# A two-layer transformer block on one core: where the first feed-forward bias is added, who makes the low parts of its hidden values, and how weights are buffered and the last stage ordered

## What is computed

```
x = x + attention(layernorm(x), ctx, mask)       # one head, masked keys
x = x + experts(layernorm(x))                     # layer 0: 4 encoder layers, each batch takes its best 2
x = x + attention16(layernorm(x), ctx)            # layer 1: 16 heads, causal
x = x + moe(layernorm(x))                         # shared expert for all, one of 8 experts for 512 tokens

encoder layer: qkv = x @ iw.T + ib ; o = softmax(q k / 4) v ; o = o @ ow.T + ob
               x = layernorm(x + o) * n1w + n1b
               ff = relu(x @ l1w.T + l1b) @ l2w.T + l2b      # 256 -> 1024 -> 256
               layernorm(x + ff) * n2w + n2b
```

## Time and profile before

| what | us |
|---|---|
| median of three runs | 782.21 (781.33 to 782.88) |
| the profiled execution, its own time | 782.31 |
| its span in the trace | 780.5 |
| PE busy in the span | 716.6 (92%) |
| DVE busy | 620.0 (79%) |
| POOL busy | 378.5 (48%) |
| ACT busy | 338.8 (43%) |
| time that ScalarE's `hh` (L1149) waited for PE | 67.8 |
| time that GpSimd's `affine2` (L2077) waited for DVE | 171.3 |

### The profile page before, as it was taken

One profiled execution on the slowest core, in us unless ns is written; L12 is line 12 of the kernel. 1 busy time (PEld: TensorE's weight loads), 2 busy tenths in 40 slices (PEclk: granted clock), 3 DMA queues, 4 the chain that ended last, 5 costly groups with the idle time before them and its releaser, 6 DMA issues.

```text
span 780.5 us, 29149 instructions
## 1 busy us (share of the span) xinstructions
PE 716.6 (92%) x11014; PEld 567.3 (73%) x11014; DVE 620.0 (79%) x1803; ACT 338.8 (43%) x711; POOL 378.5 (48%) x637
## 2 busy tenths in 40 slices
PE   5687879999999999999999999999999999987896
PEld 4466557888888888888888888888666566665684
DVE  4686665878888878888797878788889988997864
ACT  4676224343434344343434343434455555553210
POOL 4688523353535354544545353534434554547354
PEclk9797689999999999999999999999999999999798
DMA  9787200000000000000000000000112232322120
GB/s 313 253 266 274 89 2 3 3 3 3 3 3 4 3 3 3 3 3 3 3 3 4 3 3 3 3 16 10 43 57 81 78 90 90 104 89 69 38 73 7
DMA packets 24799, 40.98 MB, mean 53 GB/s; under 512 B 3871, under 2 KB 16809, under 8 KB 24411
## 3 DMA queue, kind: packets, MB, share of 16 engines
q1 hardware_dynamic: 23240, 37.13, 14.3%
q0 software_dynamic: 704, 1.71, 0.8%
q10 hardware_dynamic: 726, 0.30, 0.2%
HBM read 30.60 MB, written 8.91 MB: 51 GB/s over the span
## 4 chain that ended last, share of the span: by engine, by line
PE 69%; DVE 13%; POOL 5%; issue 4%; DMA 4%; ACT 4%; POOLq 0%; SPq 0%; ACTq 0%; DVEq 0%
PE ps L498 7%; PE ps L492 7%; PE ps L500 6%; PE ps L499 6%; PE ps L698 6%; DVE mx L1522 4%; PE ps L640 4%; PE ps L716 4%; PE ps L754 4%; PE ps L756 3%; PE ps L755 3%; DMA stage<-in_w 3%; PE ps L642 3%; PE ps L641 2%; PE ps L752 2%
## 5 line engine op out<-in xcount | busy, mean ns | idle before, releaser
L1131 ACT ACTIVATE pT<-ps 128x1024 f32<-128x1024 f32 x96 | 93.1, 1021 | 123.2 <-PE ps L698 123.2
L1522 DVE TENSOR_REDUCE mx<-ps 128x16 f32<-128x2048 f32 x48 | 109.5, 2281 | 1.0 <-PE ps L659 1.0
L2077 POOL TENSOR_TENSOR y<-y,vec 128x256 f32<-128x256 f32 x32 | 23.2, 726 | 171.3 <-DVE y L1288 171.3
L754 PE MATMUL ps<-xh,w_hi 128*128 128x128 bf16 x512 | 99.4, 219 | 0.0
L755 PE MATMUL ps<-xl,w_hi 128*128 128x128 bf16 x512 | 99.3, 219 | 0.0
L756 PE MATMUL ps<-xh,w_lo 128*128 128x128 bf16 x512 | 99.3, 219 | 0.0
L1982 POOL TENSOR_TENSOR rs<-rs,cst 128x1 f32<-128x1 f32 x132 | 75.6, 573 | 10.3
L1980 POOL TENSOR_TENSOR rs<-mv,cst 128x1 f32<-128x1 f32 x132 | 28.0, 212 | 99.7 <-DVE mv L1285 93.1
L498 PE MATMUL ps<-w_hi,hh 128*128 x256 | 69.8, 273 | 0.0
L499 PE MATMUL ps<-w_hi,hl 128*128 x256 | 69.8, 273 | 0.0
L500 PE MATMUL ps<-w_lo,hh 128*128 x256 | 69.8, 273 | 0.0
(11 more groups left out here) (361 smaller groups left out, 2436.1 us busy)
## 6 DMA issues: line engine op xcount, KB each, us to landing
stage<-in_w SPq DMA_DIRECT2D x32, 384.0 KB, 4.9
vec<-in_vec SPq DMA_DIRECT2D x4, 896.0 KB, 5.7
vec<-in_tw SPq DMA_DIRECT2D x12, 256.0 KB, 2.9
ctxc<-in_ctx SPq DMA_DIRECT2D x19, 128.0 KB, 2.2
comb<-x SPq DMA_DIRECT2D x16, 128.0 KB, 1.7
comb<-x1b SPq DMA_DIRECT2D x16, 128.0 KB
out<-x SPq DMA_DIRECT2D x16, 128.0 KB, 2.1
ytok<-t SPq DMA_DIRECT2D x14, 128.0 KB, 1.8
```

The source lines that it names most:

```text
L754: mm(dst, w(w_hi, c, j), xh[:, c, :], start=False, stop=False)
L1131: A(pT[:, 8 * a:8 * a + 8, :].rearrange("p h q -> p (h q)"), ps[:, 2 * a:2 * a + 2, :].rearrange("p g k -> p (g k)"), ACT.Exp, scale=SCALE ...
L1522: nc.vector.tensor_reduce(mx[:, :], att.rearrange("p g s k -> p (g s) k"), AX.X, ALU.max, negate=True).then_inc(m_max, 1)
```

## The change

The diff, cut to its core. "hf" is a new fp32 buffer of two halves for the hidden values after bias and ReLU; "bunit" holds the eight bias columns of a unit.

```diff
 # buffers and SyncE, first attention
+        stage_even = [vec[:, (1 + q // 2) * V_EXP + 2 * D + (q % 2) * QCH: ...] for q in range(4)]
+        def staged(i, q):
+            return stage[:, q, :] if i % 2 else stage_even[q]
             def next_quarter(i, q):
                 ...
-                sp.dma_start(stage[:, q, :], w_d[:, ds((i + 1) * ...)]).then_inc(w_in[q], 16)
+                quarter(i + 2, q)
-            for i in range(PAIRS - 1):
-                if i % 2 == 1:
-                    bias_rows(i // 2)
+            for i in range(PAIRS - 2):
+                if i == 2:
+                    sp.wait_ge(cst_ready, 1)
+                    bias_rows(0)
+                if i == 4:
+                    bias_rows(3)
                 ...
-            bias_rows(E - 1)
+            sp.wait_ge(w_lo_quarter, PAIRS - 1)
+            sp.wait_ge(w_lo_ready, (PAIRS - 1) * 3)
+            bias_rows(1)
+            bias_rows(2)
 # TensorE, hidden and second
-                    mm(dst, b1hl[:, b0:b0 + 128], row_of(e), start=True, stop=False)
                     for c in range(KC):
-                        mm(dst, w(w_hi, c, j), xh[:, c, :], start=False, stop=False)
+                        mm(dst, w(w_hi, c, j), xh[:, c, :], start=(c == 0), stop=False)
                 ...
                 if half == 1:
                     pe.wait_ge(hl_b, u + 1)
+                    pe.wait_ge(hh_a, u + 1)
+                else:
                     pe.wait_ge(hl_a, u + 1)
 # TensorE, last stage
+            def warm(n):      # n products of 512 columns into a free bank
             sh_transposes(B - 1)
+            warm(2)
             ...
             sh_z(B - 3)
+            warm(3)
             ...
             last.then_inc(d_oT, 1)
+            warm(1)
 # ScalarE, relu and its place
             def relu(u, half):
                 act.wait_ge(h_b if half else h_a, u + 1)
-                A(hh[:, 4 * half:4 * half + 4, :], ps[:, 7 - half, :]..., ACT.Relu).then_inc(hh_b if half else hh_a, 1)
+                act.wait_ge(bunit_ready, 1 + u + 1)
+                if u > 0:
+                    act.wait_ge(hl_b if half else hl_a, u)
+                for j in range(4):
+                    k = 4 * half + j
+                    last = A(hf[half][:, 128 * j:128 * j + 128], ps[:, 7 - half, 128 * j:128 * j + 128], ACT.Relu,
+                             bias=bunit[:, u % RING, k:k + 1])
+                last.then_inc(hf_ready, 1)
+                act.wait_ge(hf_ready, 16 + u * 2 + (1 if half else 2))
+                copy(hh[:, 4 * half:4 * half + 4, :], hf[half]...).then_inc(hh_b if half else hh_a, 1)
+                if attends(n):
+                    oo(n)
                 if encodes(f):
                     relu(f, 1)
-                if attends(n):
-                    oo(n)
 # VectorE
-                if encodes(f):
-                    h_low(f, 1)
             ...
-                if encodes(f):
-                    h_low(f, 0)
+                weights_quarter(i)            # now ahead of pair_stats(i + 2)
 # GpSimd
+            def h_low(u, half):
+                pool.wait_ge(hh_b if half else hh_a, u + 1)
+                tt(hl[:, 4 * half:4 * half + 4, :], hf[half]..., hh[:, 4 * half:4 * half + 4, :],
+                   ALU.subtract).then_inc(hl_b if half else hl_a, 1)
+            def unit_bias(u):
+                cols = bcols[:, ds(digit(words_pool[u // WORD], u % WORD) * B_COLS, B_COLS)]
+                nc.gpsimd.tensor_copy(bunit[:, u % RING, :], cols).then_inc(bunit_ready, 1)
             (in block)
                 if encodes(f):
                     rstd(1, n, l1_var, l1_veps, l1_rstd)
+                if encodes(n - 2):
+                    h_low(n - 2, 0)
                 ...
                     affine1(f, ex(-1))
                     x1_bias(f, 1 - slot, ex(-1))
+                if encodes(f):
+                    h_low(f, 1)
                 if encodes(n - 3):
                     rstd(2, n - 2, l2_var, l2_veps, l2_rstd)
                     affine2(n - 3, ex(-3))
+                if encodes(n + 2):
+                    unit_bias(n + 2)
 # last stage: VectorE makes last_of_equal(2) ahead of mask_tokens(3), last_of_equal(3) and
 # stored_rows ahead of mask_z(0) (before: after gated_norm(1) and gated_norm(2));
 # GpSimd gathers the rows (2, 3) of comb after the last tile's affine, not after tile 1's
```

More of the change, by code:

```diff
@@ L80 @@
 K_ALL = K_ROW + NROW
-B_QK = DFF
-B_ALL = DFF + 2 * D
+B_QK = 0
+B_ALL = 2 * D
+B_COLS = FC
+RING = 4
 def batch_of(u):
@@ L146, in encoder_kernel @@
         b1hl = sb("b1hl", [128, B_ALL], bf16)
+        bcols = sb("bcols", [128, E * B_COLS])
+        bunit = sb("bunit", [128, RING, B_COLS])
+        hf_a = sb("hf_a", [128, 512])
         cst = sb("cst", [128, C_ALL])
@@ L204, in encoder_kernel @@
         stage = sb("stage", [128, 4, QCH])
+        stage_even = [vec[:, (1 + q // 2) * V_EXP + 2 * D + (q % 2) * QCH:(1 + q // 2) * V_EXP + 2 * D + (q % 2 + 1) * QCH]
+                      for q in range(4)]
+        def staged(i, q):
+            return stage[:, q, :] if i % 2 else stage_even[q]
         kraw = vec[:, 0:K_ALL]
+        hf = (hf_a, h[:, 512:1024])
         gl = h[:, 0:12 * B * E].rearrange("p (k j) -> p k j", j=B * E)
@@ L293, in encoder_kernel @@
         x_third = c_ctx
+        w_even = (tw_in0, tw_in1, tb_in, tg_in)
+        W_EVEN = 16 * (PAIRS // 2)
         A1, D1 = B + 1, UNITS + 1
@@ L373, in _ @@
                 sp.dma_start(rows_f, b1_d[:, c0:c0 + width]).then_inc(b1_in, 16)
+            sp.dma_start(bcols[:, :], bc_d).then_inc(bcols_in, 16)
             sp.dma_start(s12_raw, sw_d[:, 0:KC * 2 * HM]).then_inc(sw_in, 16)
@@ L940, in _ @@
                 block_c(b, b % 2, ex_of(UNITS - 1)[0] if b == 1 else None)
+            def warm(n):
+                for _ in range(n):
+                    mm(ps[:, 5, :], identb[:, :],
+                       identb[:, :].rearrange("p (o k) -> p o k", o=1).broadcast_to([128, 4, 128]), start=True, stop=True)
             gathered()
@@ L1049, in weights_high @@
             def weights_high(i, q):
-                act.wait_ge(w_in[q], i * 16 + 16)
-                copy(w_hi[:, ds(i * (4 * QCH) + q * QCH, QCH)], stage[:, q, :]).then_inc(w_hi_ready, 1)
+                act.wait_ge(landed(i, q), (i // 2 + 1) * 16)
+                copy(w_hi[:, ds(i * (4 * QCH) + q * QCH, QCH)], staged(i, q)).then_inc(w_hi_ready, 1)
             def pair_exps(i):
@@ L1148, in relu @@
                 act.wait_ge(h_b if half else h_a, u + 1)
-                A(hh[:, 4 * half:4 * half + 4, :], ps[:, 7 - half, :].rearrange("p (c k) -> p c k", k=128),
-                  ACT.Relu).then_inc(hh_b if half else hh_a, 1)
+                act.wait_ge(bunit_ready, 1 + u + 1)
[7 more added lines that the diff above has]
+                act.wait_ge(hf_ready, 16 + u * 2 + (1 if half else 2))
+                copy(hh[:, 4 * half:4 * half + 4, :], hf[half].rearrange("p (c k) -> p c k", k=128)).then_inc(hh_b if half else hh_a, 1)
             def block(n, kp):
@@ L1172, in tw @@
             def tw(c, turn, j):
-                act.wait_ge(tw_in1 if j else tw_in0, turn * 16)
+                act.wait_ge(tw_in1 if j else tw_in0, W_EVEN + turn * 16)
                 copy(w_hi[:, ds(c * TCH, TCH)], tstage[:, j, :]).then_inc(tw_hi, 1)
@@ L1565, in x1_low @@
                    ALU.subtract).then_inc(x1T_split, 1)
-            def h_low(u, half):
-                dve.wait_ge(hh_b if half else hh_a, u + 1)
-                stt(hl[:, 4 * half:4 * half + 4, :], ps[:, 7 - half, :].rearrange("p (c k) -> p c k", k=128), 0.0,
-                    hh[:, 4 * half:4 * half + 4, :], ALU.max, ALU.subtract).then_inc(hl_b if half else hl_a, 1)
             def sum2(u, slot):
@@ L1827, in _ @@
             dve.wait_ge(sv_in, 32)
+            dve.wait_ge(hl_b, UNITS)
             for b in range(1, B):
@@ L1957, in _ @@
             sh_sum(B - 1)
+            last_of_equal(2)
             mask_tokens(3)
             gated(1)
+            last_of_equal(3)
+            stored_rows()
             mask_z(0)
             gated_norm(1)
-            last_of_equal(2)
             gated(2)
+            gated_norm(2)
             mask_z(1)
-            gated_norm(2)
-            last_of_equal(3)
-            stored_rows()
             for step_of, t in ((gated, 3), (mask_z, 2),
@@ L2013, in weights_low @@
                 for c in range(0, QCH, LOW):
-                    last = tt(w_lo[:, ds(w0 + c, LOW)], stage[:, q, c:c + LOW], w_hi[:, ds(w0 + c, LOW)], ALU.subtract)
+                    last = tt(w_lo[:, ds(w0 + c, LOW)], staged(i, q)[:, c:c + LOW], w_hi[:, ds(w0 + c, LOW)], ALU.subtract)
                 last.then_inc(w_lo_ready, 1)
@@ L2120, in block_c @@
                     rstd(1, b + (A1 - 1), s_var, s_veps, s_rstd)
+                if b == 1:
+                    h_low(UNITS - 1, 0)
                 if served(b + 1):
@@ L2151, in base_of @@
                 return digit(words_pool[u // WORD], u % WORD) * V_EXP
```

(2 more changed lines are left out.)

60 lines of the change are left out of this document (34 added, 26 removed).

## The result

The changed kernel takes 885.9 us (884.8 to 886.7, four runs); the kernel before took 782.1 beside it. The ratio is 1.133, 95% interval 1.131 to 1.135: slower by 104 us. The forecast was 896, the range 835 to 935.

What follows compares the result with a forecast made beforehand. PE was taken as the bound, with DVE and POOL just in time. Span 780.5 + 87 (two waits) + 36 (clock) - 6 (first attention) - 3 (last stage) = 894.5, with 1.8 around it 896 us; range 835 to 935.

Steps and rivals of the forecast that it cites:

- What bounds the kernel: Second stage: PE, busy 99.16 of 100 us, is the bound, but DVE and POOL arrive just in time.
- The bias products: TensorE, second stage: eight products fewer save at most 0.45 us a unit, 14.4 us; a good part would become waiting.
- ScalarE's half: Each relu half: four activations 1.15 us, own semaphore wait 0.1, cast 0.62; together 1.9 us against 0.60.
- The chain: From t, x1's transposes' start, through relu, h_low, rstd(2), norm2, y_low: PE waits about 2.9 us before even blocks' projection_qk.
- The second wait: Ahead of x1's transposes in every even block: PE stands still about 3.3 us, behind GpSimd's list after an odd block.
- (b): Rival: chain shorter than priced, or only one of the two stalls bites; 820 to 845 us, chance 0.12.
- The clock: Second stage: 30 idle times of 2.9 and 3.3 us lower PE's granted clock, 1.2 us each, +36 us.
- First attention: First stage: twice the buffers remove weight waits, all pairs at 7.6 us would save 9; taken -6, bounds -9 and +2.
- Last stage: Six warm products save up to 4 us, reordering up to 3, gather delays up to 2.5; taken -3, bounds -7 and +2.
- (a): Rival: the same two waits, but the clock holds; 860 us, 850 to 872, chance 0.25.
- (d): Rival: the clock stays low for most of the stage, all 81 us and dependent delays; 935 to 960 us, chance 0.08.
- (c): Rival: faster, h_low comes before norm2 is due, decided at t + 5.9; 763 us, 757 to 775, chance 0.05.

Runs made afterwards that it cites:

- low_dve: The changed kernel with both halves of h_low given back from GpSimd to VectorE, the biases staying on ScalarE: 783.1 us.
- rstd_first: The changed kernel with GpSimd's rstd(2) moved ahead of h_low(f, 1) instead of behind it: 803.1 us.
- wait_hh_a: The kernel before with one added wait: GpSimd waits for ScalarE's later half, relu(f, 0), ahead of rstd(2): 847.8 us.
- warm_fill: The changed kernel with extra TensorE products filling both stalls of every even block from block 4 on, no wait removed: 859.1 us.
- relu_plain: The changed kernel with ScalarE's four activations of 128 columns replaced by one of 512, first layer's bias left out of the computation: 859.7 us.
- no_warm: The second stage of the kernel before with the changed kernel's first and last stages, minus the last stage's six extra products: 775.5 us.
- wait_hh_b: The kernel before with one added wait: GpSimd waits for ScalarE's earlier half, relu(f, 1), ahead of rstd(2): 786.9 us.
- low0_dve: The changed kernel with only h_low(., 0) given back to VectorE, h_low(f, 1) staying on GpSimd ahead of rstd(2): 878.0 us.
- warm_proj: The changed kernel with 13 extra TensorE products ahead of projection_qk of every even block from block 4 on, none ahead of x1's transposes: 869.6 us.

## Why the prediction was right, step by step

**What bounds the kernel.** Right. DVE and POOL came just in time, and PE's 99% gave no room to either.

**The bias products** could save at most 14.4 us and gave none: nothing of the 0.45 us of a unit gets past `out_proj`, which waits for `o_low` (low_dve: at t + 6.10 as before). The prediction had "a good part"; it is all of it.

**ScalarE's half.** 1.15 us for the four activations, exactly the sum from the Exp of 128 columns; the wait for its own semaphore 0.03, not 0.1; 1.80 in all, not 1.9. GpSimd's `h_low` 1.15 (1.16), `unit_bias` 0.19 (0.3; its lower bound).

**The chain.** `hh` at t + 6.53 (predicted 6.35), `rstd(2)` ends at t + 8.53 (8.4), `projection_qk` at t + 9.91 (9.85); the wait 3.00 us (2.9). That this chain and no other makes the wait, is shown by rstd_first, which removes it by an order, and wait_hh_a, which makes it by a wait.

**The second wait**, ahead of x1's transposes: 2.55 us, predicted 3.3. The odd block is 15.83 us (416.95 to 432.78) instead of 16.3; `unit_bias` and the way from `norm2` to `affine2` are shorter. A pair with the clock held is 31.9 us (warm_fill), not 32.4: 15 × 5.3 = 80 us, not 87. Both waits are in every pair, so (b)'s case of one wait alone did not come.

**The clock: mechanism right, both factors wrong.** The term was 30 falls at 1.2 us, 36 in all. The trace of after has one fall in nearly every pair, not two: six from 300 to 500 us, with 37.5 us at half speed. The pair that starts at 296.48 has none and takes 32.3 us; the one that starts at 328.77 has two and takes 35.8. Each fall costs about twice what I took: 34.1 - 31.9 = 2.2 us, near the 2.7 of the earlier trace rows. 15 × 2.2 = 33 by the pairs, 27 by the medians of warm_fill and after. The two errors, too many falls and too cheap ones, nearly cancel: that the term came within 10 us is luck. The rule that I set beside it, that a loop which waits between bursts pays the slow clock anew after every wait (the Trainium skill, "TensorE: Matmul & The Clock Gate", section "HAM oscillation — how this bites in real kernels"), is stated there for a kernel whose waits last about 3 to 5 us, which I left out; for the shorter waits of this case it is not borne out. In wait_hh_a, with 29 waits of 1.6 to 2.4 us, the clock is at half for 3.4 of the 200 us from 300 to 500, and it falls eight times in the whole stage; in relu_plain eight of 13 pairs have a fall.

**First attention**: -3.15, predicted -6. The step that failed is "all pairs at 7.6". The maxima of pairs 0 and 7 are at 12.86 and 71.78, 8.4 us a pair instead of 8.9; only the last interval is short (4.6), most are 8.8, and the first is 10.3 where it was 7.4. The waits for weights did go: from 20 to 68 us the kernel before has this row in the view of the waits, and after the change no engine there waits for a DMA.

```profile
ACT w_hi L1032 <- DMA stage<-in_w: 16.4, 11, 3.5
```

So these waits lay mostly beside something else that sets 8.8 us a pair. What that is, no run here shows.

**Last stage**: -4.9, predicted -3. I gave the extra products up to 4 us; no_warm shows that most of the gain is the order's, and leaves 0 to 2.4 us for the products. Both ends together are worth 6 us by the medians (776.0 against 781.7), less than the 8.1 of the two traces.

**The sum** that the parts make: 780.5 + 80 + 27 - 3 - 5 = 879.5. The span is 883.0. The 80 + 27 are 2.5 more than the 104.54 of the table, since not all 15 pairs have both waits in full (the one that starts at 131.37 takes 28.9 us). The +6.05 behind the 33rd maxima was not in the sum at all: PE still waits 3.17 us (ahead of 632.54) and 1.23 us (ahead of 651.55) there, and the clock falls once more.

**The rivals.** (a), the clock held, would be warm_fill's 859, and 860 was its figure. (d), a clock that stays low for most of the stage, is far off: it is at half for 89 of the 491 us from 131 to 622. (c), faster, had the right point of decision, t + 5.9, and wait_hh_b shows it from its side.

## What to carry to other kernels

Before a step is put into an engine's list, ask what its input is waiting for and who waits for what stands behind it. Here 1.15 us of new work cost 4 to 8 us where its input was early, 16 us where its input was late but the tiny step stood ahead of it, and 95 us ahead of that tiny step, for which another engine, and behind it TensorE, came just then. The cheapest test is to move only the tiny step, or to add only the wait. And work taken from the engine that is 99% busy is worth nothing if that engine waits a little later for another one that was just in time.

## What the runs showed of the hardware beyond that

**VectorE beside GpSimd.** `norm1`, of 256 columns from SBUF to SBUF, takes 1.24 us instead of 0.41 when `h_low` runs on GpSimd beside it (411.59 against 411.43, where GpSimd's instruction ends); over all 32 units:

```profile
L1332 DVE TENSOR_SCALAR x<-t,mv,rs x32: 811/1236/1246, 113.7 to 634.5; 128x256 f32<-128x256 f32 x32
L1332 DVE TENSOR_SCALAR y<-h,mv,rs x16: 411/413/416, 152.8 to 658.6; 128x256 f32<-128x256 f32 x16
```

Columns: shortest, median and longest in ns; the second row is the same operation at a place where GpSimd waits for it. In low0_dve, where no `h_low` runs beside it, the instruction of the first row has a median of 416 ns. In the changed kernel the longer `norm1` costs nothing, since GpSimd's `affine1` starts at 412.13 anyway. The Trainium skill ("SBUF — State Buffer", section "Who interferes with whom") says that such a VectorE instruction and a GpSimd one lock each other out for a whole instruction. The end of `norm1`, 0.16 us behind that of `h_low`, agrees in kind. That only 0.16 us follow, and not the whole 0.41 of the instruction alone, the page does not say and no row explains.

**A clock that moves its fall.** With one of two waits in a pair filled (warm_proj), the fall went to the other: there the clock fell behind a wait of 2.57 us, where in the changed kernel it had held behind one of 2.55. Between 2 and 3 us the length of the wait alone does not tell whether the clock falls. Of the changed kernel's 14 waits of 2.75 to 3.04 us ahead of `projection_qk`, 13 have a fall and one of 2.85 (ahead of 306.43) has none. Of the 15 waits of 2.2 to 2.4 us there in wait_hh_a, six have one. In low0_dve, from 290 to 480 us, with waits of 3.2 to 3.4 and 2.0 to 2.2 us by turns, the clock falls behind every one. What decides between, the runs leave open.
